# Squares of layer 1's q and k moved from VectorE to GpSimd, zero products in the first slots, and one turn of q four slots later

## The reference, cut to what matters

```python
# layer 0 attention, 16 heads of 8: q and k normalised over all 128 columns, no mask
q = l2norm(x @ Wq.T); k = l2norm(x @ Wk.T); out = softmax(q k^T / (8 * temperature)) v @ proj.T + b
# layer 0 ffn: rows of x quantised to int8, one product with an int8 weight, scales, bias
# layer 1 attention: q and k get a layernorm over each head's 8 columns, gamma, beta, rope, causal mask
q = rope(layernorm8(x @ Wq.T)); k = rope(layernorm8(x @ Wk.T)); out = softmax(mask(q k^T / sqrt(8))) v @ Wo.T + bo
# layer 1 ffn: (silu(x @ Wg.T) * (x @ Wu.T)) @ Wd.T, 384 hidden columns
```

## Time and profile before

| what | value |
| --- | --- |
| median of 2 runs | 831.91 us (831.68 to 832.14) |
| the profiled execution's own time | 833.45 us |
| its span, first to last instruction | 831.4 us |
| mean granted clock of PE | 0.993 of full speed |
| PE busy / ACT busy / DVE busy / POOL busy | 803.6 / 772.3 / 540.3 / 169.9 us |

### The profile page before, as it was taken

How to read it: one execution, slowest core, us unless ns; L and a number is a source line. 1 busy time by engine, 2 the same in 40 slices (tenths; PEclk the granted TensorE clock), 3 DMA queues, 4 the chain that set the end, 5 groups by cost and what they waited for, 6 DMA issues and landing times.

```text
span 831.4 us, 18912 instructions
## 1 busy us (share of the span) xinstructions
PE 803.6 (97%) x7457; PEld 295.6 (36%) x7457; DVE 540.3 (65%) x1426; ACT 772.3 (93%) x869; POOL 169.9 (20%) x370
## 2 busy tenths in 40 slices
PE   8899999999999999999999999999999999999996
PEld 4223332333333433343333433343333343443444
DVE  4265666868867787876663677675754267785656
ACT  4899999999999999999999999999999999898972
POOL 3110000100000601033000611023200354362220
PEclk9899999999999999999999999999999999999999
DMA  5765414242602631362130421321231231071000
GB/s 144 248 225 190 177 40 146 83 141 76 242 27 88 231 140 39 99 232 78 59 133 26 150 81 39 140 90 45 72 130 51 81 110 51 27 240 53 15 14 15
DMA packets 48556, 88.74 MB, mean 107 GB/s; under 512 B 5200, under 2 KB 14544, under 8 KB 48464
## 3 DMA queue, kind: packets, MB, share of 16 engines
q1 hardware_dynamic: 47696, 85.95, 30.4%
q0 software_dynamic: 288, 1.05, 0.4%
q10 hardware_dynamic: 480, 0.48, 0.2%
HBM read 50.50 MB, written 35.65 MB: 104 GB/s over the span
## 4 chain that ended last, share of the span: by engine, by line
PE 75%; ACT 13%; DVE 7%; issue 3%; DMA 0%; ACTq 0%; DVEq 0%
PE ps L1011 37%; PE ps L989 21%; ACT probs L826 13%; PE ps L879 9%; PE ps L868 3%; PE ps L964 3%; DVE th L1421 1%; DVE hT L1422 1%; PE ps L873 1%; PE ps L1045 1%; PE ps L1053 0%; DVE sums_t L1249 0%; DVE gate_sb L1416 0%; DVE mid_part L1411 0%; DVE mid_part L1412 0%
## 5 line engine op out<-in xcount | busy, mean ns | idle before, releaser
L826 ACT ACTIVATE probs<-ps 128x1024 f32<-128x1024 f32 x800 | 749.3, 1057 | 31.0 <-PE ps L989 21.2
L1011 PE MATMUL ps<-probs,v_st 128*32 128x512 f32 (+3 forms) x3584 | 428.1, 560 | 3.2 <-issue 2.4
L989 PE MATMUL ps<-q_st,k_st 32*128 32x512 f32 (+3 forms) x1792 | 266.3, 460 | 7.8 <-ACT probs L826 7.2
L989 PEld LDWEIGHTS ps<-q_st,k_st 32*128 32x128 f32 x1792 | 120.1, 182 | 288.0 <-ACT probs L826 221.7
L734 POOL TENSOR_SCALAR_AFFINE_SELECT probs<-probs 128x256 f32<-128x256 f32 x256 | 103.8, 428 | 144.7 <-ACT probs L826 143.0
L1011 PEld LDWEIGHTS ps<-probs,v_st 128*32 128x32 f32 x3584 | 78.7, 108 | 110.4 <-issue 74.2
L702 POOL COPY v_st<-v_all 128x256 f32<-128x256 f32 (+1 forms) x65 | 29.1, 456 | 343.2 <-PE ps L1011 334.9
L1249 DVE STREAM_TRANSPOSE sums_t<-ps 128x512 f32<-128x512 f32 x32 | 22.9, 716 | 45.3 <-PE ps L1011 44.7
L1390 DVE COPY mid_qkv<-ps 128x384 f32<-128x384 f32 x32 | 17.8, 557 | 35.8 <-PE ps L879 34.8
L964 PE MATMUL ps<-yTp,w_hid 128*128 128x512 f32 x84 | 31.2, 453 | 4.1 <-DVE gate_sb L1416 2.5
L1390 DVE COPY prep_qkv<-ps 128x384 f32<-128x384 f32 x24 | 13.4, 558 | 27.1 <-PE ps L879 26.4
(11 more groups left out here) (190 smaller groups left out, 641.3 us busy)
## 6 DMA issues: line engine op xcount, KB each, us to landing
k_st<-parts_scratch SPq DMA_DIRECT2D x46, 512.0 KB, 3.6
parts_scratch<-mid_part SPq DMA_DIRECT2D x34, 512.0 KB, 4.4
q_st<-parts_scratch SPq DMA_DIRECT2D x62, 256.0 KB, 3.9
parts_scratch<-prep_part SPq DMA_DIRECT2D x28, 512.0 KB, 4.8
k_st<-parts_scratch SPq DMA_DIRECT2D x17, 256.0 KB, 2.9
xT<-in_xT SPq DMA_DIRECT2D x8, 256.0 KB, 4.4
x_all<-in_x SPq DMA_DIRECT2D x8, 256.0 KB, 5.3
out<-yo SPq DMA_DIRECT2D x7, 256.0 KB, 2.3
```

Source lines behind the costliest of these rows:

```text
L826: nc.scalar.activation(probs[:, k % PS, :, 0:w], slot(k)[:, :, 0:w], ACT.Exp).then_inc(probs_ready, 1)
L989: last_ = mm(slot(k)[:, e, at:at + n], k_st[row, p % KB, kt * P:(kt + 1) * P], q_st[row, p % KB, lo:HALF], start=True, stop=not shifted)
L1011: last_ = mm(acc[HR * h:HR * (h + 1), lo:HALF], v_st[:, p % VB, kt, h, :], probs[:, (2 * s + h // 2) % PS, h % 2, at:at + n], start=FIRST[ ...
```

## The change

`mid` loses its unit `square`. POOL does it after its copy of v, and counts it in a new semaphore `squared`; DVE's `norms` of a `mid` chunk waits for that. The planner's list loses the unit and its 1.7 us and gets no entry for the wait. The turn of q of chunk 1 goes from slot 1 to slot 5 (`scale_q` stays). `BETWEEN` is allowed from slot 7 on only. After each of the score tiles 3, 4, 5 and 6 PE computes two products of zeros into the bank of the sums, before any sum is there.

```diff
-      [(e, n, 0) ... ("square", "norms", "rs1", "rs2", "scale", "rope0", "rope1", "rope2", "rope3")] + QKT      # MID
+      [(e, n, 0) ... ("norms", "rs1", "rs2", "scale", "rope0", "rope1", "rope2", "rope3")] + QKT
...
-    out[1] += FIRST_KEYS[1:]
+    out[1] += FIRST_KEYS[1:2]
+    out[5] += FIRST_KEYS[2:]
...
-            if s < NS - 1 and max(one, act) + 0.45 < sums - GAIN:
+            if BRANCHED <= s < NS - 1 and max(one, act) + 0.45 < sums - GAIN:
...
-    WARM = (10, 4, 0, 22)
+    WARM = (10, 4, 0, 22, 7)
...
         def store_v(name, c):
             pool.wait_ge(qkv_copied[name], c + 1)
             g_.tensor_copy(v_all[...], buffers(name, c)["qkv"][:, :, 2 * C:3 * C]).then_inc(v_stored[name], 1)
+            if name == "mid":
+                qk = job["mid"]["qkv"][:, :, 0:2 * C]
+                g_.tensor_tensor(job["mid"]["sq"][:], qk, qk, ALU.mult).then_inc(squared, 1)
...
                     if k % 2 and s in BETWEEN:
                         sums(s - 1)
+                    if k < WARM[4]:
+                        keep_warm(2, ACC)
...
             elif what == "norms":
+                if name == "mid":
+                    dve.wait_ge(squared, c + 1)
                 ch.link(v.tensor_reduce(per(0), by(sq[:]), AX.X, ALU.add))
```

More of the change, by code:

```diff
@@ L117 @@
       [("pe", "normT", 0)] + [("pe", "qkv", t) for t in range(TC)] + \
-      [("dve", n, 0) for n in ("square", "norms", "rs1", "rs2", "scale", "rope0", "rope1", "rope2", "rope3")] + QKT
+      [("dve", n, 0) for n in ("norms", "rs1", "rs2", "scale", "rope0", "rope1", "rope2", "rope3")] + QKT
 LAST = LN_UNITS + [("pe", "normT", 0)] + \
@@ L489, in program @@
     v_in, more_v_in = sem("v_in"), sem("more_v_in")
+    squared = sem("squared")
     scores_ready = sem("scores_ready")
```

## The result

The changed kernel takes 863.3 us (862.4 to 864.2, two runs) where the kernel before took 831.9: a ratio of 1.037 with an interval of 1.035 to 1.039 (the ratio gives 30.5 us, the two medians 31.4). The prediction was 7.1 us slower, 839 us with 829 to 846. The sign was right, the size was not, and the time lies outside the range.

The account below looks back on a forecast made before the run. PE (97% busy) and ACT (93%) were taken to bound the kernel in turns. A gain of 3.2 us at the start and a loss of 10.3 us behind the squares made 831.9 + 7.1 = 839 us, range 829 to 846.

Parts of the forecast that it names:

- The start (-3.2): First slots: zero products hold PE's clock and both ACT waits, 1.77 and 1.40 us, go; 3.2 us gained.
- DVE waits in its read of that turn, and has nothing behind it before slot 7: Slot 5, q's turn moved there: DVE's later read delays nothing, so the move has no cost.
- The square on POOL: Eight squares moved from DVE, 1.66 us each, to POOL, taken at 2.5 us each, up to 4.5 contended.
- The chunks (+10.3): Behind the eight squares: DVE's waits before `norms` make reads and turns late; 10.3 us lost in all.
- Chunks 3 and 5: DVE's read ends 2.6 us late for PE's `gate` 0; less 0.6 us of cushion, 2.0 us lost each, 4.0 together.
- 3.1 us of standing still instead of 1.66 us of work: DVE at `norms`: 0.6 us for POOL's copy of v plus 2.5 us for its square replace DVE's own square.
- this case: Chunks 0 and 2: planner moves the turn a slot forward, to 133.11; stall 2.4 us, but 1.0 each taken.
- the cushions of 0.6 us (chunks 3 and 5) and 1.2 us (chunk 4): Lateness behind these squares that ACT's tiles in stock, or a slot without side stage, would absorb.
- Rival 1: Waits behind the squares are absorbed by order and cushion, only the start's gain shows: 828.7 us, up to 831; chance 0.25.
- Rival 2: The clock falls in the first slots all the same: 10.3 us lost without gain, 842 us or a little over; chance 0.10.
- Rival 3: Full lateness behind the squares, no cushion, `rs1` ahead of reads, POOL and DVE slowing each other: 850 us; chance 0.05.
- Rival 4: Planner rearranges the last 130 us by luck: 2 or 3 us either way in every case; no chance of its own.

## Why the prediction was wrong

**The start (-3.2): right in itself, with a hole beside it.** No gap before the eighth and ninth exponential, a clock of 1.00 to 38 us, and 3.8 us gained once the branch is out of the way. The failed step is "DVE waits in its read of that turn, and has nothing behind it before slot 7". Behind it stands the branch. The slots were counted, but not what the engine itself must do between two units. The cost was 6.5 us, so that the start as it stands loses 3.1 us. The Trainium skill, Runtime: NRT & Kernel Launch, section Instruction fetch mechanics, says that a taken branch to code that isn't loaded yet forces a fetch by DMA before the engine can go on. The trace agrees, with the 5.79 us of "issue" above, which go when the branch is early; that section gives no price and names no DMA traffic beside it.

**The square on POOL: 2.5 us was too much.** It takes 1.89 us. The wait is then 2.62 us and not 3.1. The estimate from the Trainium skill, GPSIMD Engine Reference, section 3.1, was 2.3 us; it is nearer than mine, and the measurement is below both. The overlap was right in kind, the size was not: this error works against the loss, and so hides part of the next. The other side of the comparison was off too. DVE's 1.66 us is not what its square takes alone. The same instruction on the chunks of layer 0, in the kernel before:

```profile
L1210 DVE TENSOR_TENSOR prep_qk<-prep_qkv x6: 1225/1444/1662, 49.1 to 344.0; 128x1024 f32<-128x1024 f32 x6
```

The three of 1.66 us (74.18, 146.15, 266.36) start within 0.03 us of POOL's copy of v, as all eight squares of layer 1 do; the three of 1.23 us have no such copy beside them. So 0.43 us of the 1.66 came with POOL's copy.

**The chunks (+10.3): this is the step that failed.** Term by term, with PE's stall and ACT's gaps from the rows above (ACT's with the small gaps that follow):

| chunk | predicted | PE's stall | ACT's gaps | clock behind it |
| --- | --- | --- | --- | --- |
| 0 and 2 | 2.0 | 1.84 + 1.55 | 3.80 + 2.76 | falls, holds |
| 1 | 2.0 | 3.24 | 5.57 | falls |
| 3 and 5 | 4.0 | 2.53 + 1.90 | 2.86 + 1.90 | holds, holds |
| 4 | 0.7 | 2.93 | 4.21 | falls |
| 6 | 0.2 | 2.04 | 3.34 | falls |
| 7 | 1.4 | 2.52 | 5.14 | falls |
| sum | 10.3 | 18.6 | 29.6 (25.8 over the kernel before) | |

The places were right: `norms` right behind the copy, PE stopped by DVE behind every square. Chunks 3 and 5, which were worked out row by row with the full lateness, came out at 4.8 for 4.0. The others failed in three ways.

First, the wait was netted against the removed square ("3.1 us of standing still instead of 1.66 us of work"), and in chunks 3, 4 and 5 a cushion was taken off as well. But the planner had already spent the 1.66 us: it moved `norms` and `rs1` ahead of reads and turns (chunks 1 and 4), and the turn of k forward to a slot where PE asks for it earlier (chunks 0 and 6). In chunk 0 `norms` comes only 0.8 us later behind the copy than before (2.62 us where it was 1.84), and yet PE stands still for 1.84 us: the turn of k now has the slot of the product that stood at 133.11. The prediction had weighed just this case, at 2.4 us, and took 1.0. In chunk 6, given 0.2 us because no side stage followed, PE asks for the turn 12.2 us behind the start of the copy, where before it came 20.0 us behind it. The same order without the wait costs only 3.5 us, and with it 24.3 us more. So the whole wait counts, not the difference. Eight times the forecast 3.1 us, less 3.2 for the start, would have given 831.9 + 24.8 - 3.2 = 853.5 us. The steps as measured are 831.9 - 3.8 + 3.5 + 24.3 + 6.5 = 862.4 us, against 863.3; being differences of kernels in a row they must add up, so this shares the loss out and proves nothing more.

Second, the cushions of 0.6 us (chunks 3 and 5) and 1.2 us (chunk 4) were not there when they were needed. In chunk 5 PE's stall and ACT's gap are both 1.90 us: ACT had nothing in stock beyond what PE's restart used up.

Third, the clock. The prediction looked for it in the first slots alone, as its second rival. It fell behind five of the eight stalls; in those five ACT lost 22.1 us (3.80 + 5.57 + 4.21 + 3.34 + 5.14) for 12.6 us of PE's stalls, in the other three 7.5 for 6.0. What PE did before each fall was to stand still for 1.8 to 3.2 us; but it stood still for 2.53 us in chunk 3 too, and the clock held, and with the early branch it held behind chunk 1's 3.24 us and fell behind chunks 3 and 5. Which of the stalls it follows changed when an earlier one was mended. Why stays open.

**The rivals.** Rival 1, the waits absorbed, is refuted for this order (24.3 us lost for 21.0 us waited); told of the wait, the planner comes to 831.1 us. Rival 2 is refuted: the clock was 1.00 from 18 to 38 us. Rival 3 had the right mechanism in part, full lateness without a cushion and `rs1` ahead, and was given 0.05. Its other part, POOL and DVE slowing each other at the square, did not happen: the square took 1892 to 1894 ns all eight times, and DVE stood still beside it. With `norms` held back it took 1892 to 1897 ns, but there too DVE had no operation on two SBUF tensors beside it, so how far the two would slow each other was not tested. Rival 4, luck in the last 130 us, is small: ACT's idleness before its exponentials there is 8.6 us before and 10.6 after, chunk 7's gaps included.

**What stays open** beside the clock: why the loading of DVE's code took so long (that the place of the flag's read and the branch is the cause was shown; no run had the stores alone moved, and the first packet took 3.0 us or more without them). And why the kernel with `norms` held is still 2.1 us above the one with the squares on DVE. Their profiled spans differ by 0.9 us only (828.4 and 827.5), with the same 18.1 us of ACT's idleness released by PE.

## What to carry to other kernels

When work leaves an engine and a wait takes its place, and a planner writes the order, count the whole wait: the planner gives the freed time to other units, and knows nothing of the wait until it is told. One condition in the planner won 25.7 us back; the squares on POOL then gain nothing over DVE's, and don't lose much. And when an engine's last step before a branch is moved, ask how soon the first instruction behind the branch is needed.

## What the runs showed of the hardware

- Behind a branch DVE stood still for 5.79 us, marked "issue"; two packets of an instruction queue moved through the DMA engines 3.9 us after the branch, beside 1 MB of stores, and the first instruction began 1.9 us behind them. Taken 12 us earlier, where DVE had nothing to do, the branch cost nothing.
- A stall of PE of 2 to 3 us can cost up to twice its length (ACT's gaps 1.4 to 2.1 times the stall): the sums behind it take 1.93 us instead of 1.06 while the clock is at its lower level. It happened behind five of eight stalls, and one stall of 3.24 us was followed by the lower clock in one kernel and not in another.
- POOL squares 128x1024 of one tensor in 1.89 us, less than twice the 1.27 us of its addition of two operands at 128x512. DVE takes 1.23 us for it alone and 1.66 us beside a copy of 0.61 us that POOL starts at the same time; POOL's copy stays at 0.61 us.
